# One-hots from memory, a fused rescale and queries head by head in a graph network kernel

## The reference

```python
x = ln(x + x @ rotations(edge_weight, src, dst))        # one 256x256 matrix out of 50000 plane rotations
x = ln(x + gated_attention(x, ...))                      # below
x = ln(x + filter_conv(x, ...))                          # below
x = ln(x + mean over edges with this src of (x @ W + b)[dst])

def rgat(x, src, dst, etype, W, Q, K, b, heads, ch):     # called three times: heads 4, 4, 1, ch 128
    xw = einsum("ni,rio->rno", x, W)                     # a table for each type
    alpha = leaky_relu(xw[etype, dst] @ Q + xw[etype, src] @ K, 0.2)
    alpha = segment_softmax(alpha, dst)
    return segment_sum(xw[etype, src] * alpha, dst) + b

def filter_conv(h):
    Wf = ssp(ssp(edge_attr @ m1 + b1) @ m2 + b2) * cutoff(edge_weight)
    return ssp(segment_sum((h @ aw)[src] * Wf, dst) @ o1) @ o2     # ssp: softplus - log 2
```

## Time and profile before

| | us |
|---|---|
| median of 3 runs | 6792.22 |
| profiled execution | 6790.51 |
| its span, first to last instruction | 6788.7 |
| PE busy | 4443.6 |
| POOL busy | 3598.5 |
| DVE busy | 3307.0 |
| ACT busy | 1900.9 |

### The profile page before, as it was taken

One profiled execution on the slowest core, in us unless ns is written; L12 is line 12 of the kernel. 1 busy time (PEld: TensorE's weight loads), 2 busy tenths in 40 slices (PEclk: granted clock), 3 DMA queues, 4 the chain that ended last, 5 costly groups with the idle time before them and its releaser, 6 DMA issues. The chain is left out here.

```text
span 6788.7 us, 80592 instructions
## 1 busy us (share of the span) xinstructions
PE 4443.6 (65%) x17924; PEld 3192.7 (47%) x17925; DVE 3307.0 (49%) x7696; ACT 1900.9 (28%) x4413; POOL 3598.5 (53%) x2941
## 2 busy tenths in 40 slices
PE   5699620884766779476667444458777878775553
PEld 5588510542555544355557433334555555443332
DVE  6576456213555532455553233342777777523334
ACT  0122100001554511255441122211555555410000
POOL 0244310466766637676656788831444444228885
PEclk6799855897887889787786555555999999875555
DMA  0000012224655523565542222212222222223332
GB/s 7 24 11 11 8 37 76 55 66 110 169 153 134 150 60 73 134 168 145 140 124 46 45 46 45 45 53 63 59 58 59 60 59 58 61 75 84 84 84 74
DMA packets 487810, 511.57 MB, mean 75 GB/s; under 512 B 307562, under 2 KB 372575, under 8 KB 487289
## 3 DMA queue, kind: packets, MB, share of 16 engines
q0 software_dynamic: 359872, 381.65, 23.3%
q1 hardware_dynamic: 127670, 127.35, 6.7%
HBM read 440.64 MB, written 65.22 MB: 75 GB/s over the span
## 5 line engine op out<-in xcount | busy, mean ns | idle before, releaser
L1200 POOL DMA_INDIRECT sum_gx_sb<-scratch_xw,keep_k_row_step_sb x1296 | 1612.9, 1244 | 598.7 <-issue 358.4
L1291 PE MATMUL sum_a_ps<-sum_gx_sb,sum_sel_sb 125*125 125x258 f32 (+1 forms) x4320 | 1231.4, 450 | 581.1 <-ACT sum_gx_sb L1233 261.0
L1291 PEld LDWEIGHTS sum_a_ps<-sum_gx_sb,sum_sel_sb 125*125 125x125 f32 x4320 | 950.9, 246 | 779.7 <-issue 586.8
L1233 ACT ACTIVATE sum_gx_sb<-sum_gx_sb,sum_wt_sb 125x129 f32<-125x129 f32 x3024 | 897.4, 388 | 454.5 <-DVE sum_wt_sb L1422 454.5
L2342 POOL DMA_INDIRECT filter_gx_sb<-scratch_h,keep_k_src_step_sb x432 | 519.5, 1203 | 665.1 <-DVEq L2483 519.1
L2770 POOL DMA_INDIRECT source_gx_sb<-scratch_h,source_grouped_sb x432 | 533.9, 1236 | 156.1 <-issue 117.6
L2782 PE MATMUL source_s_ps<-source_gx_sb,source_sel_sb 125*125 125x257 f32 x864 | 376.9, 612 | 310.4 <-DMA source_gx_sb<-scratch_h,source_grouped_sb 310.4
L1109 POOL DMA_INDIRECT scratch_grouped<-keep_k_value_sb,keep_k_place_sb x400 | 475.5, 1189 | 124.0 <-issue 124.0
L2388 PE MATMUL filter_ps<-filter_m_sb,filter_h_sb 128*125 128x256 f32 x1760 | 442.5, 409 | 34.1 <-DVE filter_f_sb L2452 34.1
L2782 PEld LDWEIGHTS source_s_ps<-source_gx_sb,source_sel_sb 125*125 125x125 f32 x864 | 250.5, 304 | 436.8 <-issue 171.1
L2388 PEld LDWEIGHTS filter_ps<-filter_m_sb,filter_h_sb 128*125 128x125 f32 x1760 | 346.2, 202 | 181.4 <-issue 126.0
(11 more groups left out here) (503 smaller groups left out, 7318.7 us busy)
## 6 DMA issues: line engine op xcount, KB each, us to landing
sum_gx_sb<-scratch_xw,keep_k_row_step_sb POOLq DMA_INDIRECT x1296
scratch_xw<-gate_xsb_sb SPq DMA_DIRECT2D x50, 253.9 KB
scratch_xw<-attend_xsb_sb SPq DMA_DIRECT2D x50, 253.9 KB
filter_ea_sb<-in_ea_t SPq DMA_DIRECT2D x444, 24.4 KB
filter_gx_sb<-scratch_h,keep_k_src_step_sb POOLq DMA_INDIRECT x432
source_gx_sb<-scratch_h,source_grouped_sb POOLq DMA_INDIRECT x432
sum_mk_sb<-scratch_masks SPq DMA_DIRECT2D x72, 93.9 KB
scratch_grouped<-keep_k_value_sb,keep_k_place_sb POOLq DMA_INDIRECT x400, 3.8
```

Of the source, the lines that this page charges most:

```text
L1200: nc.gpsimd.indirect_dma_start(out=gx[:, q, j, :], out_offset=None, in_=table, in_offset=bass.IndirectOffsetOnAxis(ap=keep["row_step"][:, ...
L1233: last = nc.scalar.activation(here, here, ACT.Copy, scale=wt[q][:, h, j:j + 1])
L1291: last = mm(psa[b][0:P, half, 0:BF], sel[:, p, j, :], gx[:, q, at, half * BF:(half + 1) * BF], **flags)
```

## The change

- nodes_gate makes the one-hots of all 36 blocks, one operation of 125 x 1500 for each, behind the other work of a tile; a ring of three buffers; ACT's queue stores them to a new tensor (scratch_hots, 125 rows of 54000 words).
- The attentions and the filter load them instead of making them: SP loads a part (125 rows of 2000 bytes) when PE has summed the same part two blocks before, PE waits for the three loads of its block. iota is no longer loaded there. The filter's loads of edge attributes are reordered around them.
- With pick left only the product of the fourth head, in parts 0 and 1; in part 2 ACT scales all four heads.
- rescale and the first addition of a block become grow_and_add, one operation for each head: sum times factor plus PSUM.
- The queries are spread head by head, with type 1 minus type 0 times type plus type 0; PE starts on a head when it is there; ACT copies into qs. Of agg, DVE clears the tiles that the spreading does not use before it, ACT the others behind it.
- DVE, PE and SP are unrolled by 6 blocks in all attentions.
- The lists src_tile and dst_tile are released before the gate stage.

```diff
@@ attention
-    act_heads = 3 if H == 4 else 1
+    shared = 2 if H == 4 else 0
-    turn = 6 if H == 4 else 3
+    turn = 6
-    sel = mem.sb("sel", [P, T // HF, HF, P])
+    sel = mem.sb("sel", [P, 2, T // HF, HF, P])
+    spread_tiles = -(-(NEC * PART + 2 * NEC * H * P) // 516)
@@ SP
+            def load_hots(s, q, p):
+                sp.dma_start(sel[:, q, p].rearrange("p j n -> p (j n)"), dr["hots"][:, bass.ds((s * T + p * HF) * P, HF * P)]).then_inc(
+                    hot_in[q], 16)
+            def after(s, u):
+                if not isinstance(s, int) or s + 3 < NS:
+                    sp.wait_ge(mask_used, s + 1)
+                    load_masks(s + 3, u % 3)
+                if not isinstance(s, int) or s + 2 < NS:
+                    for p in range(PARTS):
+                        sp.wait_ge(summed, s * T + (T + (p + 1) * HF))
+                        load_hots(s + 2, u % 2, p)
@@ ACT
-                    for h in range(act_heads):
+                    for h in range(H - 1 if j < shared * HF else H):
...
+            for h in range(H):
+                act.wait_ge(q_summed, h + 1)
+                nc.scalar.copy(qs[:, :, h], psw[h % 2][0:P, 0:KS]).then_inc(q_taken, 1)
+            nc.scalar.activation(agg[:, 0:spread_tiles, 0:F], zero[:].unsqueeze(2).broadcast_to([P, spread_tiles, F]),
+                                 ACT.Copy).then_inc(cleared, 1)
@@ PE
+                pe.wait_ge(hot_in[k], pairs * (16 * PARTS))
                 for p in range(PARTS):
-                    pe.wait_ge(parted, s * PARTS + p + 1)
+                    if p < shared:
+                        pe.wait_ge(parted, s * shared + p + 1)
@@ DVE
+            vec.memset(agg[:, spread_tiles:NT + 1, 0:F], 0.0)
...
-            for c in range(NEC):
+            for h in range(H):
                 for r in range(2):
-                    for h in range(H):
+                    for c in range(NEC):
...
+                vec.tensor_tensor(by_type[1][:, :, h], by_type[1][:, :, h], by_type[0][:, :, h], ALU.subtract)
+                dve.drain()
                 vec.tensor_tensor(by_type[1][:, :, h], by_type[1][:, :, h], keep["type"][:], ALU.mult)
+                dve.drain()
+                vec.tensor_tensor(by_type[0][:, :, h], by_type[0][:, :, h], by_type[1][:, :, h], ALU.add).then_inc(spread, 1)
...
             def pick(s, q, p):
-                dve.wait_ge(summed, s * T + p * HF + HF)
-                vec.tensor_tensor(sel[:, p], iota[0:P, 0:P].unsqueeze(1).broadcast_to([P, HF, P]),
...
-                                  ALU.is_equal)
-                if act_heads < H:
+                if p < shared:
...
-                dve.drain()
-                dve.nop().then_inc(parted, 1)
...
+            def grow_and_add(n, tile, steps):
+                dve.wait_ge(summed, n + steps + T)
+                here = agg[:, bass.ds(tile, 1), 0:F].rearrange("p o f -> p (o f)")
+                for h in range(H):
+                    at, inside = h * (W + 1), h % (H // banks) * (W + 1)
+                    last = vec.scalar_tensor_tensor(here[:, at:at + W + 1], here[:, at:at + W + 1], fac[:, h:h + 1],
+                                                    psa[0][0:P, h // (H // banks), inside:inside + W + 1], ALU.mult, ALU.add)
+                last.then_inc(added, steps)
+                dve.drain()
...
-                rescale(firsts[0])
...
-                pick(s, q, 2)
@@ nodes_gate, ACT and DVE
+    def blocks_at(t):
+        return range(NS * t // NT, NS * (t + 1) // NT)
...
+            def store_hots(t):
+                for s in blocks_at(t):
+                    act.wait_ge(hot_made, s + 1)
+                    act.dma_start(dr["hots"][:, s * T * P:(s + 1) * T * P], hots[:, s % 3].rearrange("p j n -> p (j n)")).then_inc(
+                        hot_out[s % 3], 16)
...
+                for j, link in enumerate((take_x1, hidden, gate, take_x0)):
+                    link(g)
+                    if GN * (g - 1) + j >= 1:
+                        store_hots(GN * (g - 1) + j - 1)
...
+            def make_hots(t):
+                for s in blocks_at(t):
+                    if s >= 3:
+                        dve.wait_ge(hot_out[s % 3], 16 * (s // 3))
+                    vec.tensor_tensor(hots[:, s % 3], iota[:].unsqueeze(1).broadcast_to([P, T, P]),
+                                      keep["dloc"][:, s * T:(s + 1) * T].unsqueeze(2).broadcast_to([P, T, P]),
+                                      ALU.is_equal).then_inc(hot_made, 1)
@@ filter_sum, DVE, PE and SP
-                    vec.tensor_tensor(sel[:], iota[0:P, 0:P].unsqueeze(1).broadcast_to([P, HF, P]),
...
+                    pe.wait_ge(hot_in[q], i * 16 + 16)
...
+                    sp.wait_ge(hid, 2 * i + q + 4)
+                    load(i * U2 + (q + 5) * HF, 1 - q)
+                    sp.wait_ge(summed, 2 * i + q + 1)
+                    load_hots(2 * i + q + 2, q)
```

More of the change, by code:

```diff
@@ L1306, in _ @@
                 last.then_inc(q_summed, 1)
+            pe.wait_ge(q_taken, H)
             turn_scores(0)
@@ L1329, in block_of @@
                     turn_scores(s + 2)
-            with pe.Fori(0, NS // 3 - 1) as i:
-                for q in range(3):
-                    block_of(3 * i + q, q, 2)
-            for q in range(3):
-                block_of(NS - 3 + q, q, 2 - q)
+            with pe.Fori(0, NS // 6 - 1) as i:
+                for u in range(6):
+                    block_of(6 * i + u, u % 3, u % 2, 3 * i + (u // 2 + 1), 2)
+            for s in range(NS - 6, NS):
+                block_of(s, s % 3, s % 2, s // 2 + 1, min(2, NS - 1 - s))
         @block.vector
         def _(dve):
-            dve.wait_ge(landed, 48)
+            dve.wait_ge(landed, 32)
             vec.memset(ones[:], 1.0)
+            vec.memset(zero[:], 0.0)
             vec.memset(state_f[:, 0:1], -BIG)
             vec.memset(state_b[:], -BIG)
-            vec.tensor_scalar(other[:], keep["type"][:], -1.0, 1.0, ALU.mult, ALU.add)
+            dve.drain()
+            dve.nop().then_inc(blank, 1)
+            vec.memset(agg[:, spread_tiles:NT + 1, 0:F], 0.0)
             dve.wait_ge(first_in, 16 * NEC)
@@ L1452, in add_part @@
                 with dve.If(spans[p] < 1):
-                    add(n, p, firsts[p], HF)
+                    if p:
+                        add(n, p, firsts[p], HF)
+                    else:
+                        grow_and_add(n, firsts[0], HF)
                 with dve.If(spans[p] > 0):
@@ L1456, in add_part @@
                     for j in range(HF):
-                        add(n + j, (p + j) % 3, tiles[j], 1)
+                        if p or j:
+                            add(n + j, (p + j) % 3, tiles[j], 1)
+                        else:
+                            grow_and_add(n, tiles[0], 1)
             def block_of(s, i, q, ahead):
@@ L1631, in nodes_gate @@
          "x0t_made", "x0_turned", "x0_made", "x0_out", "projected", "taken", "q_out"))
+    iota, hots = mem.sb("iota", [P, P]), mem.sb("hots", [P, 3, T, P])
+    iota_in, hot_made, hot_out = mem.sem("iota_in"), mem.sem("hot_made"), [mem.sem(f"hot_out{q}") for q in range(3)]
     grouped, put = mem.sem("grouped"), mem.sem("put")
@@ L1845, in take_x0 @@
                     x0_made, 1)
+            def store_hots(t):
[3 more added lines that the diff above has]
+                        hot_out[s % 3], 16)
             act.wait_ge(ready, 1)
             for g in range(LAST + 1):
-                take_x1(g)
-                hidden(g)
-                gate(g)
-                take_x0(g)
+                for j, link in enumerate((take_x1, hidden, gate, take_x0)):
+                    link(g)
+                    if GN * (g - 1) + j >= 1:
+                        store_hots(GN * (g - 1) + j - 1)
+            for t in range(GN * LAST - 1, NT):
+                store_hots(t)
+            for q in range(3):
+                act.wait_ge(hot_out[q], 16 * (NS // 3))
         @block.vector
@@ L2329, in filter_sum @@
          "f2_made", "log2_made", "ms_made", "summed", "added"))
-    x_in, e_in = [mem.sem(f"x{q}") for q in range(2)], [mem.sem(f"e{q}") for q in range(2)]
+    x_in, e_in, hot_in = ([mem.sem(f"{n}{q}") for q in range(2)] for n in ("x", "e", "hot"))
     vec, mm = nc.vector, nc.tensor.matmul
@@ L2859, in build @@
         dr[name] = nc.dram_tensor("scratch_" + name, shape, F32, kind="Internal").ap()
+    dr["hots"] = nc.dram_tensor("scratch_hots", (P, KS * P), F32, kind="Internal").ap()
     dr["grouped"] = nc.dram_tensor("scratch_grouped", (P * KS, 2), I32, kind="Internal").ap()
@@ L2874, in build @@
         keep = edge_lists(keeper)
-        with phase("order") as mem:
-            edge_order(nc, mem, dr, keep)
-        with phase("bucket") as mem:
-            source_order(nc, mem, dr, keep)
+        with phase("ends") as lists:
+            for n in ("src_tile", "dst_tile"):
+                keep[n] = lists.sb(n, [P, ET], I32)
+            with phase("order") as mem:
+                edge_order(nc, mem, dr, keep)
```

(2 more changed lines are left out.)

112 lines of the change are left out of this document (53 added, 59 removed).

## The result

The changed kernel takes 6856.8 us (median of 4 runs, 6844.7 to 6861.1), the kernel before 6795.4 (4 runs on the same chip, 6788.7 to 6800.3): ratio 1.0086, 95% interval [1.0070, 1.0102]. The forecast was 6748, faster; it is 0.9% slower. The profiled execution took 6844.7, its span 6842.8: 54.1 us more than the span before.

| from ... to | before | after | difference | forecast |
|---|---|---|---|---|
| begin ... POOL's first row gather of attention 1 | 1599.1 | 1684.6 | +85.5 | +115 |
| ... first weights of attention 1 | 65.7 | 54.2 | -11.5 | -19 |
| 35 blocks of attention 1 | 748.9 | 774.8 | +25.9 | -20 |
| ... first weights of attention 2 | 408.3 | 399.4 | -8.9 | -19 |
| 35 blocks of attention 2 | 749.0 | 780.9 | +31.9 | -20 |

What follows compares the result with a forecast made beforehand. Wide attentions were taken as bound partly by POOL's gather rate, partly by the loop DVE, ACT, PE, DVE. Terms -62 - 38 - 40 + 115 - 18 = -43 took 6790.5 to 6748 us; range 6630 to 6830.

Steps and rivals of the forecast that it cites:

- (c): Blocks of the wide attentions: comparisons leave DVE, -30 us, against +10 for the one-hot loads; -20 each, -40 for both.
- +10 for gathers that land later: Wide attentions: the loads of one-hots delay gathers on nearly full DMA engines; +10 us for each attention.
- rival 2: Wide attentions: one-hot loads fill the five DMA engines and gathers queue; +102 us, about 6890; chance 0.20.
- the quick half of the prediction: Attention 1: 18 of 35 blocks lay between 17.1 and 18.4 us; gain there some 5 us, 22 in slow ones.
- 18.9 us of engine time in a block: Wide attentions, five engines: gathers 11.6, masks 0.6 and one-hot loads 6.7 us, of about 20.8 us a block.
- some 5 us of slack behind the gathers: Wide attentions: DVE's scores for block s+2 can be some 5 us late before anything waits.
- DVE's wait for gathers over 60 us: Sign that the forecast is wrong: this wait in a wide attention, 5 us before, passes 60.
- (a): Filter: the comparison leaves DVE's chain, 0.60 us for each of 108 groups; -62 us, bounds -45 and -70.
- (b): Start of the wide attentions: scoring begins near 1637 instead of 1657.7; -19 us each, -38 for both.
- (d): Gate stage: stores of one-hots, 125 rows on five DMA engines, lengthen it; +115 us, bounds 0 and +170.
- (e): Third attention: POOL's remaining waits for PE and most of its gather stretch go; -18 us, bounds -8 and -35.
- (f): PE's loop body grows from 3 blocks to 6, code fetched in larger turns; 0, within 10 us either way.

## Why the prediction was wrong

The step that failed is in (c): the loads of one-hots, "+10 for gathers that land later". They cost 70 and 85 us of the loops (774.8 - 704.5, 780.9 - 696.2). This is rival 2's mechanism and about its size: it gave up the 30 us that the rest of the change was to gain in a loop, and 1.5 us more in each of 35 blocks, 82 in all.

Where they cost it is seen when the blocks that were short before (18 of 35, under 19 us, the quick half of the prediction) are added up apart from the other 17, the long ones. In attention 1 the short blocks took 319 us before, 311 without loads, 352 with them; the long ones 430, 394 and 423. In attention 2 it is 320, 310 and 357 against 429, 387 and 424. The long blocks take less than before even with the loads; the whole loss lies in the short ones.

Two things were wrong in the term. First, 18.9 us of engine time in a block were compared with the mean block of 20.8, though rival 2 set them against POOL's 18.1 and the quick half last 17.1 to 18.4. Second, 18.9 is too small. It added up the gathers as they ran without loads beside them, 11.6 us, and the loads at the rate of another transfer, 6.7 us (27.0 MB at the 112 GB/s of the load of x). In the third attention, at a DMA share of 0.33, a row of 2000 bytes took 105 ns, 7.9 us of each of five engines for a block. Beside the gathers of attention 1 it took 118 ns, 8.9 us, and the gathers took 13.0 us (55.4% of 774 us for 33 blocks). With the masks these are over 22 us by shares that count some per cent high, more than the mean block of 20.8 too. That DVE would have some 5 us of slack behind the gathers was assumed, and no row showed it; they came 8 us later (12.6 for 4.7).

Five engines are not the whole of it: on sixteen, at a share of 0.83, the loads still cost 30 and 41 us (734.4 - 704.5, 737.1 - 696.2), so somewhat less than half of the 70 and 85 is there wherever the loads run. One of the forecast's signs of being wrong came true, DVE's wait for gathers over 60 us (63.9); but it stands at 60.7 in the kernel with 128 rows, so it was no good sign.

- (a) *Filter*: -55 for -62. Right; 10.0 us a group, not 9.85.
- (b) *Start*: -21.5 where nothing is loaded in the wide attentions (65.7 to 44.2 us), for -19. Right; the one-hot loads that start there, which I left out, take back 8 to 10. In the changed kernel -11.5.
- (c) *Blocks without the loads*: -44 and -53 for -30, of which the comparisons are 32 and 42 (736.2 - 704.5, 738.0 - 696.2) and the rest 13 and 11. Right in mechanism, too small, and in the long blocks: these gave 36 and 42 us where I had 22, the short ones 8 and 11 where I had 5.
- (d) *Gate*: +85.5, mean of seven +93, for +115. The mechanism is shown: no stores, no growth. The five engines are full throughout, as forecast, and the shares sum as forecast: 226 us of one-hots (16.5% x 16 x 428 / 5), 200 of the other direct transfers, 30 of q0, 456 where I had 459 to 484. But the stage has 428: the shares count high by some 6%, and I took 4% off half the sum and then added idle time that hardly occurs. DVE waits for its row stores for 141 us of it (79 before), not most of the time.
- (e) *Third attention*: -13, with what lies around it -15, for -18. Right; the mean gather is 1.20.
- (f) *Longer body*: bodies of three blocks gave 1.0105 for 1.0086, and with the starts 829 and 832 us for 829 and 834: nothing gained. Right.

With the measured sizes, gate 93, starts 2 x (-21.5 + 9), loops +26 and +32, third and filter -15 and -55, the sum is +56. The rule of the Trainium skill ("DMA: Bandwidth & Descriptors", section "Why a DMA increments its semaphore by 16 and not by 1") held in all seven row counts and on both queues; the 6.7 us of the loads rest on it as the gate's term does. Not the rule failed, but the rate of 2000-byte rows, the adding up, and what the sum was compared with.

## What to carry to other kernels

Before work moves from an engine to the DMA engines, add up the busy time of the fullest DMA engine in the shortest period of the loop, not of all sixteen in the mean one, and take it as a lower bound: here gathers and loads each took more beside the other (13.0 for 11.6 us, 8.9 for 7.9) than apart. A row count like 125 puts a transfer on five of them; 128 rows with padding, or 112 and 13, are cheap to write and were worth some 165 and 55 us here. And ask what the move itself gains: with 128 rows the wide loops took 734 and 737 us, with DVE's own comparisons 736 and 738. The best kernel here shares the work: it loads two thirds of the one-hots and lets DVE, which has room, make the rest.

## What the runs showed of the hardware

The number of engines of a transfer can be counted in a profile: beside its rows a transfer has one small packet for each engine, in all seven row counts. Engines at full share do not have one rate. Rows of 6000 bytes went at 26 GB/s for each engine with 128 and with 125 rows, 24 with 100, but 19 with 112, 15 with 120 and 121 and 13 with 64 (the rates above by 16, 5, 10, 16, 15, 11 and 16 engines). Why is open. Rows of 2000 bytes on five engines went at 19 GB/s for each in the third attention (105 ns) and 17 in the first (118 ns). Loads on all sixteen engines still stretch the gathers beside them: q0's share of the 35 blocks, for equal bytes, went from 56.3% of 705 us with no loads to 63.0% of 734 us with loads of 128 rows, 397 to 462 us.
